# A decoder's Mamba layer in a two-stream merge: the sum, the decays and the inputs of a state placed a fraction of a state later

## The reference

```python
def _selective_scan(u, delta, A, Bm, Cm, D):
    def step(h, inp):
        d, b, c, ut = inp
        dA = jnp.exp(d[:, :, None] * A)
        h = dA * h + (d * ut)[:, :, None] * b[:, None, :]
        y = jnp.einsum('bdn,bn->bd', h, c)
        return (h, y)
    ...
    return ys.transpose(1, 0, 2) + u * D
...
x_f = _mamba(xn, *margs)
x_r = jnp.flip(_mamba(jnp.flip(xn, 1), *margs), 1)
y = jnp.concatenate([x_f, x_r], axis=-1) @ dim_reduce_w.T + dim_reduce_b
```

## Time and profile before

| What | Value |
|---|---|
| Median of 3 runs | 4764.98 us (4752.53 to 4768.23) |
| Profiled execution, its own time | 4766.72 us |
| its span, first to last instruction | 4764.2 us |
| PE, busy | 3496.6 us (73%) |
| DVE, busy | 2955.6 us (62%) |
| ACT, busy | 1970.0 us (41%) |
| POOL, busy | 1234.1 us (26%) |
| DMA, mean over the span | 69 GB/s |

### The profile page before, as it was taken

The page is one execution under the profiler, slowest core; times in us unless marked ns, Lnnn a source line. Parts: engine busy times, 40 slices in busy tenths (PEclk is TensorE's granted clock), DMA queues, the critical chain, the costliest instruction groups (busy, mean ns, idle before and its releaser), DMA issues. The chain is left out here.

```text
span 4764.2 us, 69288 instructions
## 1 busy us (share of the span) xinstructions
PE 3496.6 (73%) x25546; PEld 2337.3 (49%) x25546; DVE 2955.6 (62%) x6919; ACT 1970.0 (41%) x3470; POOL 1234.1 (26%) x1568
## 2 busy tenths in 40 slices
PE   5868867666878878665886887856589698685674
PEld 3645635334665555433575654533357465352353
DVE  4436874884554785577545488477654548738646
ACT  2423545343343444543344355434235335443333
POOL 0001451550000243253000045145100005516410
PEclk7989978777988988777898998877789799786776
DMA  7110121313121021032122112122211200211321
GB/s 237 46 47 14 39 81 42 103 55 106 66 79 62 28 76 58 29 130 73 47 100 69 39 36 81 45 88 84 104 56 52 98 10 28 80 54 45 117 101 49
DMA packets 174905, 328.00 MB, mean 69 GB/s; under 512 B 13260, under 2 KB 114988, under 8 KB 173740
## 3 DMA queue, kind: packets, MB, share of 16 engines
q1 hardware_dynamic: 174572, 323.59, 20.1%
HBM read 231.87 MB, written 91.67 MB: 68 GB/s over the span
## 5 line engine op out<-in xcount | busy, mean ns | idle before, releaser
L1881 PE MATMUL bank<-sb_big,sb_weights_const 128*128 128x512 f32 x512 | 376.6, 826 | 333.9 <-DVE sb_big L2119 333.2
L1434 POOL TENSOR_TENSOR sb_rs<-sb_ve,sb_weights_const 128x4 f32<-128x4 f32 x112 | 113.4, 1012 | 1757.6 <-DVE sb_ve L1420 1757.3
L1997 POOL TENSOR_TENSOR sb_big<-sb_big 128x512 f32<-128x512 f32 x384 | 496.4, 1307 | 244.9 <-DVE sb_big L2097 244.3
L1958 ACT ACTIVATE bank<-sb_big,sb_Aneg 128x512 f32<-128x512 f32 x512 | 351.7, 689 | 497.4 <-DVE sb_big L2114 392.3
L1252 DVE TENSOR_REDUCE sb_small<-bank 128x4 f32<-128x308 f32 (+1 forms) x512 | 265.9, 523 | 344.5 <-PE bank L967 340.9
L2114 DVE TENSOR_TENSOR_SCAN sb_big<-bank,sb_big 128x512 f32<-128x512 f32 x384 | 464.6, 1210 | 6.6 <-ACT bank L1958 6.3
L988 PE MATMUL bank<-sb_big 128*77 128x128 bf16 (+1 forms) x2560 | 358.1, 234 | 83.7 <-DMA sb_big<-key_parts 30.3
L988 PEld LDWEIGHTS bank<-sb_big 128*77 128x77 bf16 (+1 forms) x2560 | 274.2, 117 | 140.2 <-issue 89.8
L967 PE MATMUL bank<-sb_big 128*128 128x77 bf16 (+1 forms) x2048 | 187.4, 227 | 179.5 <-DMA sb_big<-query_parts 114.2
L1677 PEld LDWEIGHTS bank<-sb_weights_L1f,sb_big 128*128 128x128 f32 x2048 | 257.3, 191 | 109.0 <-issue 104.9
L1137 ACT ACTIVATE sb_big<-bank 77x512 f32<-77x512 f32 (+1 forms) x352 | 207.9, 593 | 228.3 <-PE bank L1009 152.4
(11 more groups left out here) (344 smaller groups left out, 8111.7 us busy)
## 6 DMA issues: line engine op xcount, KB each, us to landing
sb_big<-query_parts SPq DMA_DIRECT2D x160, 512.0 KB, 6.5
sb_big<-state_rows SPq DMA_DIRECT2D x128, 512.0 KB, 3.8
query_parts<-sb_big SPq DMA_DIRECT2D x120, 384.0 KB, 3.3
sb_big<-key_parts SPq DMA_DIRECT2D x64, 512.0 KB, 8.9
sb_big<-context_key_parts SPq DMA_DIRECT2D x64, 308.0 KB, 3.6
key_parts<-sb_big SPq DMA_DIRECT2D x48, 384.0 KB, 4.1
context_key_parts<-sb_big SPq DMA_DIRECT2D x48, 231.0 KB, 4.1
sb_big<-masked_key_parts SPq DMA_DIRECT2D x32, 308.0 KB, 3.5
```

The costliest lines, as they stand in the source:

```text
L1881: pe.matmul(m.bank[s][2][:, :], m.const["ident"], M.h(s, 2 * (n % 2)), start=n == 0, stop=n == NS - 1)\
L1958: act.activation(M.dA(s, half), M.dl(s, half), ACT.Exp, scale=m.Aneg[:, NS * half + n:NS * half + n + 1])\
L1997: pool.tensor_tensor(M.h(s, 2 * (n % 2) + half), M.b_rows(s, n // 2)[:, n % 2, :], M.du(s, half), ALU.mult)\
```

## The change

Five due times of Mamba's states change, no instruction is added or removed.

```diff
@@ mamba_pe
         for n in range(NS):
-            yield M.scan_at(way, n, 0.6)
+            yield M.scan_at(way, n, 0.9)
             pe.wait_ge(*g.at("sc_d", (way, n, "out", 0)))
@@ mamba_act
         for n in range(NS):
             for half in range(2):
-                yield M.at(way, 0.13) if n == 0 else M.scan_at(way, n - 1, 0.4 + 0.5 * half)
+                yield M.at(way, 0.13) if n == 0 else M.scan_at(way, n - 1, 0.6 + 0.5 * half)
@@ mamba_pool
         for n in range(NS):
             for half in range(2):
-                yield M.at(way, 0.115) if n == 0 else M.scan_at(way, n - 1, 0.2 + 0.4 * half)
+                yield M.at(way, 0.115) if n == 0 else M.scan_at(way, n - 1, 0.4 + 0.4 * half)
```

## The result

| | Median | Lowest to highest | Runs |
|---|---|---|---|
| before | 4764.48 us | 4752.53 to 4768.23 | 4 |
| after | 4693.46 us | 4693.24 to 4698.4 | 4 |

(The run before has one execution more here than in the table ahead of the prediction.) The ratio is 0.9858, with a 95% interval of 0.9839 to 0.9876: 71 us or 1.4% faster (on the medians). The profiled execution took 4693.38 us, its span is 4691.6, and the mean granted clock is 0.834, against 0.833 before.

The account below looks back on a forecast made before the run. DVE was taken to bound the sixteen stretches of Mamba states, with 155 us idle there. The sum's -26 us (3 x 7.0 + 4.7), decays and inputs 0 and new waits +3 made -23: 4742 us, range 4718 to 4766.

Parts of the forecast that it names:

- What bounds, and the places: Sixteen Mamba stretches: DVE is the bound, and time is won where it waits for the other stream behind a sum.
- PE's 333 less by some tens only: PE's 333.2 us of waits before the sum L1881 would fall by some tens of us only.
- The halves: Some DVE waits behind sums counted by half, PE nearly full or ACT between: 7.0 us a pass instead of 10.0.
- Decays and inputs at 0: Moving ACT's decays L1958 and Pool's inputs L1997 was counted as no gain, 0 us.
- DVE's busy time "unchanged": Sixteen stretches: DVE's order and busy time stay, only its idle time falls, from 155 to some 130 us.
- What a sum's place can give: Cap on each DVE wait's gain, no more than the sum's place can give; of L1286's 3.2 us, 1.0.
- Passes alike, the last one less: Gain of the sum per pass: 7.0 us in each of the first three, 4.7 in the last.
- New waits, 3 of 0 to 15 us: Cost of all new waits of the three edits, taken as 3 us, between 0 and 15.
- B: Sum: nothing given back, 37 us, plus 7.5 from the head start at each pass's first stretch; 4721 us, chance 0.15.
- C: No change: the edit moves less, DVE waits return later in the same chain; 4756 us, chance 0.33.
- D: Slower by late decays on ACT: DVE loses 0.3 us at each of 167; 4792 us, chance 0.07.
- E: Slower by PE's clock: the first stretch falls from 0.96 to 0.72; some 4826 us, chance 0.02.

Follow-up runs that it names:

- pe_only: Kernel before with only PE's sum moved, 0.6 to 0.9, decays and inputs as before: 4705.86 against 4756.27 us, ratio 0.9891.
- last_early: The whole change, but the last state's sum of each way stays at 0.6: 4705.09 against 4759.22 us, ratio 0.9884.
- first_state: Kernel before with the sum at 0.9 for the first state of each way only: 4757.64 against 4755.53 us, ratio 1.0006.
- whole_again: The whole change run once more, beside the other kernels on the same chip: 4694.53 against 4760.06 us, ratio 0.9861.
- narrow_early: Kernel before with 128 of the 512 columns summed, at the old place 0.6: 4724.5 against 4755.53 us, ratio 0.9944.

## Why the prediction was wrong in size

**What bounds, and the places: right.** DVE bounds the stretches, its order is untouched, and the gain is in the waits of DVE that stand behind a sum: L1273, L1286, L729 and L1201 wait less. In the second pass 13.0 us of DVE's waits are gone at the lines that the forecast named, anywhere in the pass: L1273 4.4, L1286 3.1, L729 2.1, L1201 1.9, L1241 1.0, L1252 0.6. "PE's 333 less by some tens only" was wrong: it fell by 117 us, since 164 moved sums take more than tens with them. That was no term of the sum, and the fall of 76 us for ACT without any gain shows how little such a number says.

**The halves: wrong.** The step that failed is "half" for waits where PE is nearly full or ACT stands between, which made 7.0 of 10.0 us a pass. The edit that it priced is the sum, and the sum alone (pe_only) shortens the four stretches of the second pass by 1.4, 3.3, 2.4 and 3.6 us, where 1.05, 2.1, 1.5 and 2.3 were forecast and 2.1, 3.2, 2.0 and 2.7 would have been the full amounts. Over the sixteen it is 38.6 us: forecast 26, in full 37. So the full amounts were right in sum and the discount was not. It had been argued and had no row. Stretch by stretch the fit is looser: something was given back in the first one, the 1.0 us at L742.

**Decays and inputs at 0: right alone, wrong beside the sum.** Neither gives anything alone (0.9995, 1.0005, both 0.9996). With the late sum the stretches become 53.5 us shorter and not 38.6: 15 us that the sum of terms had at nothing. Eight of them are the first stretches' 3.4 us for 1.4, with the decays, and three are L2185, with the inputs. By the medians the two bring 12 us, with intervals that overlap. The terms were added one by one, and an edit worth nothing by itself can be worth something when another engine no longer ends the same chain.

**DVE's busy time "unchanged": wrong by 7 us.** L1195 and L2185 became shorter in three passes, where they no longer start just behind an instruction of Pool. The prediction took a step's length as fixed and looked for gains in waits alone.

**What a sum's place can give: too low for one wait.** L1286's 3.2 us were put down to one sum, 1.0. The wait is gone altogether after the change, from 1723 to 1811. L1040 stands at the end of a chain of PE and ACT steps, each of which had passed a sum, so it can gain more than one length; which of them gave it was not traced.

**The ways' ends: left out.** 12.5 of the 66.0 us in the four passes lie between the sixteen stretches, and with the sum alone 10.7 of 49.3. The prediction said "Outside these stretches nothing is reordered", and read DVE's waits in the four windows alone. But the last sum of a way stands at the stretch's end and passes up to 16 matmuls of the other stream, and steps behind the last state come sooner with it. The lines below are the maximum of the other stream's router (L1526), DVE's copy of a projection of Mamba's input (L2035) and the product with ACT's gate at the end of Mamba (L2139). DVE's waits from 1842 to 1980 before:

```profile
DVE sb_small L1526 <- PE bank L1485: 4.8, 1, 4.8
DVE sb_big L2035 <- PE bank L1835: 4.7, 2, 3.7
DVE sb_big L2139 <- ACT sb_big L1971: 3.3, 2, 2.4
```

and the stretch that answers to it after, from 1810 to 1949:

```profile
DVE sb_small L1526 <- PE bank L1485: 4.6, 2, 4.3
DVE sb_big L2035 <- PE bank L1835: 3.5, 2, 3.3
...
DVE sb_big L2139 <- ACT sb_big L1971: 1.8, 2, 0.9
```

With L1199 and L755 these lines give 5.7 us in the second pass, of which 4.8 are left when other waits there are counted too. The last sum is part of it (last_early). "The end of a way reads the last sum too" stood in the prediction, as a cost alone; it was a gain as well.

**Passes alike, the last one less: right in shape.** 17.9, 19.8, 18.4 and 9.9 us by the starts of DVE, where 7.0 and 4.7 were forecast.

**New waits, 3 of 0 to 15 us: right in size.** L2119 waits 1.3 us more for broadcasts, L2126 1.0 more for the last sum, L2114 0.2 more for decays.

**The mechanism: in part misnamed.** The prediction spoke of the wait for the product and priced the length in the same breath ("PE waits 1.66 us for the product, sums for 1.87 us"). The runs tell the two apart: seven tenths of the sum's gain or more is its length, and the place of the wait is the rest, which may be nothing.

**The rivals.** B's "nothing is given back" was right in sum and its head start wrong (first_state, 1.0006): with 37 us in full and without the 7.5 it would have said 4728. C fell with the halves. D fell: L2114 waits 6.5 us for decays, and 6.4 even with them two tenths later again. E fell as well: the first stretch keeps its 0.96 and the run its 0.834. Something of E is in the last pass (a stretch at 0.64 that had 0.72 before) and in the fourth stretch of the second: 0.69 where the earlier trace rows has 0.77, and yet PE's longer busy time there, 57.15 for 52.90 us, didn't keep that stretch from being 2.5 us shorter. In the second execution of the same kernel (whole_again) it has 0.75 and the third stretch 0.70 for 0.76, so the clock of one stretch differs between executions by as much.

**The arithmetic once more**, with what was measured: 26 us of waits were forecast; the halves kept back 11 more, and the sum gave 1.6 beyond the full amounts; decays and inputs beside the sum are 15, the time between the stretches 12.5. Together they are the 66 us of the four passes. Of these 46.5 are DVE's idle time in the stretches, 7.1 its busy time there. The 6.5 us elsewhere are what two executions differ by there (4.1 with whole_again, -4.0 with pe_only), and no part of the change as far as these runs show. All in all 72.6, the difference of the spans, 4764.2 - 4691.6.

## What to carry to other kernels

Where one engine serves two streams in a fixed order, price a step of low urgency by its own length, not only by its wait, and put it just ahead of a wait that can't be avoided: there it costs little or nothing. One place further, behind that wait, the gain was gone here. When you add up such a gain, take the waits of the bounding engine over everything that the reordered part reaches, the ends of loops too, and don't discount by a half for which you have no row. Compare before and after between the same instructions, not in windows set by eye: here such windows hid 20 of 53 us. A large fall in the waits of an engine off the critical path proves nothing either way: here 76 us of ACT's waits went for no time at all.

## What the runs showed of the hardware

Less work on PE went with a lower granted clock. With the sum cut from 512 columns to 128, the mean over a run was 0.811 to 0.817 in six runs, and 0.809 to 0.817 in six with the short sum late, against 0.828 to 0.835 in those of the kernel before beside them. From 100 to 455 us, where no sum runs, it is 0.92 in the profiles of the kernel before and of narrow_early alike. The kernel with a quarter of the sum's columns at 0.9 took 4719 us and the one with all of them 4706. That the lower clock is the reason for this is inferred from these rows; no run here held the clock and changed only the columns.

A step of DVE that reads and writes SBUF tiles alone can be held up by one of Pool that started just before it: L1195 took 1.76 us where Pool's L1331 had started 0.05 us earlier and 0.68 where it started 0.23 us later, and L2185 up to 1.37 us behind a Pool input and 0.34 with none beside it. DVE's scans, which read the decays from PSUM, show nothing like it: all 384 with their state in sb_big before took 1.15 to 1.22 us, with Pool busy for 955 of the 1440 us of these stretches. No wait in a profile shows such a loss, since it stands in the length of the step. That is why the whole change won 7 us which no count of waits could find.
